# A graph-attention kernel on one core: third tile's masks ahead of the second table, x by rows in eight pieces, shorter flag

## The chip, the cores and the metric

One core of one Trainium2 chip. The metric is the device time of one execution in microseconds (us), as the median of three runs.

## What is computed

Cut to what matters (N = 4096 nodes, 128 channels, `adj` a 4096x4096 int32 matrix, sparse, of 64 MB):

```python
in_fts = W @ x.T
f1 = (w1 @ in_fts).T + b1              # one number per row
f2 = (w2 @ in_fts).T + b2              # one number per column
logits = f1 + f2.T                     # 4096 x 4096
bias = where(adj > 0, 0, -1e9)
coefs = softmax(leaky_relu(logits, 0.01) + bias, axis=-1)
y = x + coefs @ x
out = (y - mean(y)) / sqrt(var(y) + 1e-5)
```

## The kernel before

**The method.** leaky_relu has two slopes, so exp(leaky_relu(f1+f2)) is a product of a factor of the row and one of the column on either side of the sign of f1+f2. The kernel builds two tables of x scaled by the column's factor, `bt[:, 1]` ("minus", made first) and `bt[:, 0]` ("plus"), each with its low part beside it (258 columns, float16). For each tile of 128 rows it makes two masks of `adj`, one for each sign, and TensorE multiplies mask by table: 32 matmuls of 258 columns for each mask, 64 for a tile, 2048 for the 32 tiles (line 1091, `edge_sums`).

**One tile's way.** SyncE and ScalarE each load half of the tile's 2 MB (`load_near`, `load_far`, lines 277 to 280) into one of four buffers `nat`; the buffer is free again when the tile four back has been cast (`cast_done`). VectorE casts it to bytes (`cast`, L743), combines it with the signs that ScalarE makes (`signs`, L474, four instructions; `combine`, L748), transposes it (`turn`, L756: this is the minus mask) and derives the plus mask (`plus`, L761). TensorE sums both. ScalarE copies the sums out (`evacuate`, L616), and once per four tiles VectorE normalises (`moments`, L850 to L880), which reads x by rows, `xn`. Tiles 4 to 31 run so in loops, in pairs, each engine in program order.

**The start.** Tiles 0 to 3 are written out by hand in every engine's program, interleaved with the making of f2 (`f2_products` on VectorE, `f2_sums` on ScalarE, L495, two blocks of four columns by TensorE), f1 (`f1_columns` on TensorE from the transposed x; `spread_f1`, L710, on VectorE), the statistics (`turn_stats`, `widen_stats`, `stat_max`, `stat_out`), and the two tables. A table has four chunks; a chunk is scaled (`scale_x`, L732, on VectorE; `scale_act`, L518, or `scale_first`, L504, on ScalarE), its high part rounded by ScalarE (`split_x`, L542) and its low part formed by VectorE (`low_x`, L738). `gram` (L1103) sums squares of the minus table for a statistic. x itself lies in the storage of tile 2's and 3's masks (`xl` is `msk[:, 2:4]`), so `turn(2)` must come after chunk 1 of x has been used for both tables, `plus(2)` after chunk 0, `turn(3)` and `plus(3)` after chunks 3 and 2. The transposed x lies in the storage of `xn`, so x by rows can be loaded only after the last `f1_columns`.

**The order before** on VectorE (L792 to L839): scale minus chunks 0, 1; cast, combine tile 0; low 0; turn 0; scale 2; low 1, 2; f1; cast 1; low 3; combine 1; statistics; turn 1; scale plus chunks 2, 3; plus 0, 1 and low 0 to 3 of the plus table; then cast, combine, turn, plus of tile 2, and of tile 3. TensorE: tile 0 minus, gram, tile 1 minus, plus of tiles 0 and 1, then tile 2 minus (waits for `turn(2)`), and so on.

**x by rows and the flag.** GpSimd loads all of `xn` in four transfers of 512 KB (L379) once f1 is done and tile 1 is cast. GpSimd also computes whether the data's range allows the fast way, in twelve small operations after the rows' factors (L383 to L409), and writes `flag`; every engine reads it after its part of tile 3 (`fast`), SyncE already before it loads tile 7.

Of the kernel before, what the change touches and what calls it, by code (L numbers as in the profile page):

```python
# [16 lines left out]
P = 128  # L17
SQ = 32
# [24 lines left out]
def gat_kernel(nc, x, adj, W, w1, b1, w2, b2, out):  # L43
# [24 lines left out]
    with ExitStack() as ctx:  # L68
# [14 lines left out]
        junk = sb("junk", [P, KB * D], BF16)  # L83
# [70 lines left out]
        F2_PE = (0, 2)  # L154
        F2_AT = (FIRST * KB, NK - FIRST * KB)
# [6 lines left out]
        f2_made = sem("f2_made")  # L162
# [3 lines left out]
        y1_act = sem("y1_act")  # L166
        xl_in = [sem(f"xl_in{i}") for i in range(BCH)]
        xn_in = sem("xn_in")
# [119 lines left out]
        def _(sp):  # L288
# [8 lines left out]

            sp.dma_start(wsb[:, :], W).then_inc(w_in, 16)
# [8 lines left out]
            with sp.If(go):  # L307
# [23 lines left out]
            with sp.Else():  # L331
                for c in range(QT):
                    sp.wait_ge(nat_in[c], 16 * A * (2 if c < AHEAD else 1))
# [15 lines left out]
        def _(pool):  # L349
# [34 lines left out]
            pool.wait_ge(gst_ready, 2)  # L384
# [11 lines left out]
            pool.tensor_tensor(rng[:, 0:1], gst[:, 0:1], gst[:, 1:2], ALU.add).then_inc(rng_step, 1)  # L396
            pool.tensor_scalar(rng[:, 1:2], gst[:, 0:1], gst[:, 1:2], None, ALU.max).then_inc(rng_step, 1)
            pool.wait_ge(rng_step, 2)
            pool.tensor_tensor(rng[:, 1:2], rng[:, 1:2], gst[:, 2:3], ALU.add).then_inc(rng_step, 1)
            pool.tensor_scalar(rng[:, 0:1], rng[:, 0:1], F2_SPAN, None, ALU.is_le).then_inc(rng_step, 1)  # L400
            pool.tensor_scalar(rng[:, 2:3], gst[:, 3:4], (SCALE * X_MAX) ** 2, None, ALU.is_le).then_inc(rng_step, 1)
            pool.tensor_scalar(rng[:, 3:4], gst[:, 3:4], (SCALE * X_MIN) ** 2 * N, None, ALU.is_ge).then_inc(rng_step, 1)
            pool.wait_ge(rng_step, 6)
            pool.tensor_scalar(rng[:, 1:2], rng[:, 1:2], F_ABS, None, ALU.is_le).then_inc(rng_step, 1)
            pool.tensor_tensor(rng[:, 2:3], rng[:, 2:3], rng[:, 3:4], ALU.mult).then_inc(rng_step, 1)
            pool.wait_ge(rng_step, 8)
            pool.tensor_tensor(rng[:, 0:1], rng[:, 0:1], rng[:, 1:2], ALU.mult).then_inc(rng_step, 1)
            pool.wait_ge(rng_step, 9)
            pool.tensor_scalar(flag[:, :], rng[:, 0:1], rng[:, 2:3], None, ALU.mult).then_inc(flag_ready, 1)  # L409
# [47 lines left out]
        def _(act):  # L457
# [13 lines left out]
            def signs(t, c, between=None):  # L471

                for g in range(G):
                    ins = act.activation(sgn[:, c, g * JA:(g + 1) * JA], f2b[:, :], ACT.Sign,  # L474
                                         bias=nf1l[:, bass.ds(G * t + g, 1)], scale=-1.0)
                    if g == 1 and between:
                        between()
                ins.then_inc(sign_ready, 1)
# [6 lines left out]
            def f2_copy(i):  # L485

                b = F2_PE[i]
                bank, at = (0, F2_AT[0] + b * KB) if b < FIRST else (7, F2_AT[1] + (b - FIRST) * KB)
                act.wait_ge(f1_made if b < FIRST else f2_made, 1)
                act.activation(f2l[:, b * KB:(b + 1) * KB], ps[:, bank, at:at + KB], ACT.Copy).then_inc(f2l_act, 1)  # L490

            def f2_sums(n0, n1):
                act.wait_ge(xv_ready, 3)
                for n in range(n0, n1):
                    ins = act.activation(junk[:, (n - n0) * D:(n - n0 + 1) * D], xv[:, n * D:(n + 1) * D], ACT.Copy,  # L495
                                         accum_out=f2l[:, n:n + 1])
                ins.then_inc(f2l_act, 1)

            def scale_first(n0, n1):

                act.wait_ge(cs_ready[1], 1)
                for n in range(n0, n1):
                    h, i = n // CN, n % CN
                    ins = act.activation(ybuf[:, h, i], xl_chunk(h)[:, i], ACT.Copy, scale=cs[:, 1, n:n + 1])  # L504
                ins.then_inc(y1_act, 1)
# [27 lines left out]
            def split_x(m, h):  # L533
                if m == 0 and h < 2:
                    act.wait_ge(y_act, h + 1)
                elif m == 0:
                    act.wait_ge(y_ready[0], h - 1)
                elif h == BCH - 1:
                    act.wait_ge(y1_act, 2)
                else:  # L540
                    act.wait_ge(y_ready[1], h + 1)
# [6 lines left out]
            load_far(1, 1)  # L548
            xT_out(2)
            f2_copy(0)  # L550
            f2_sums(2 * CN, 2 * CN + KB)
            f2_copy(1)
            load_far(2, 2)
            act.wait_ge(b12_made, 1)
            act.activation(b12[:, :], ps[:, 6, D + 2:D + 3], ACT.Copy).then_inc(b12_ready, 1)
            act.wait_ge(f2l_ready, 4)
# [4 lines left out]
            scale_first(3 * CN, 3 * CN + KB)  # L561
            xT_out(4)
            act.wait_ge(f2b_ready, 1)
            act.wait_ge(nf1l_ready, 1)
            signs(0, 0, between=lambda: xT_out(5))
            load_far(3, 3)
            split_x(1, 0)
            xT_out(6)
# [3 lines left out]
            split_x(1, 1)  # L572
# [3 lines left out]
            scale_first(3 * CN + KB, NK)  # L576
            split_x(1, 2)
            signs(1, 1, between=lambda: split_x(1, 3))
            rows_out()
            scale_act(0)  # L580
            split_x(0, 0)
            act.wait_ge(cast_done, 2)
            load_far(QT + 1, 1)
            scale_act(1)
            split_x(0, 1)
            split_x(0, 2)
            split_x(0, 3)
            act.wait_ge(nf1l_ready, 2)
            signs(2, 2)

            def next_tile():
                act.wait_ge(cast_done, 3)
                load_far(QT + 2, 2)

            signs(3, 3, between=next_tile)
# [91 lines left out]
        def _(dve):  # L687
            def f2_products(i, n0, n1, s0=None):
# [6 lines left out]
                                  vsb[:, None, 0:D].to_broadcast([P, w, D]), ALU.mult).then_inc(xv_ready, 1)  # L695
                dve.wait_ge(xv_ready, i + 1)
# [38 lines left out]
            def low_x(m, h):  # L735
                part = slice(h * CN, (h + 1) * CN)
                dve.wait_ge(hi_ready[m], h + 1)
# [39 lines left out]
            f2_products(0, KB, 2 * KB)  # L777
            f2_products(1, 3 * KB, 4 * KB)
            f2_products(2, 2 * CN, 3 * CN, 2 * CN + KB)
            f2_products(3, 3 * CN, 4 * CN)  # L780
            dve.wait_ge(f2l_ready, 4)
            dve.wait_ge(f2l_act, 3)
            dve.tensor_reduce(stat[:, 0:1], f2l[:, :], AX_X, ALU.max)
            dve.tensor_reduce(stat[:, 1:2], f2l[:, :], AX_X, ALU.min, negate=True).then_inc(stat_ready, 1)
            dve.wait_ge(consts_ready, 2)
            dve.wait_ge(b12_ready, 1)
            spread_f1(0, 0, FIRST * KB, 0, 0)
            f2_rows()
# [228 lines left out]
        def _(pe):  # L1017
# [19 lines left out]
            def f1_columns(b):  # L1037
# [10 lines left out]
                if b == F2_PE[-1]:  # L1048
                    ins.then_inc(f2_made, 1)
# [168 lines left out]
```

## Time and profile before

| | us |
|---|---|
| median of 3 runs | 277.59 |
| the runs | 276.06 to 278.6 |
| the profiled execution, its own time | 275.19 |
| its span, first to last instruction | 273.5 |
| around the span | 1.7 |

An instruction's name is its line, engine and what it writes and reads; "idle before" is how long its engine had nothing to do ahead of it, and the arrow names what released it. TensorE has two rows, matmuls (PE) and weight loads (PEld), which overlap. The duration of a matmul in the rows is that from its start to its end, and several are in flight, so a rate is read from the time that a whole group takes.

### The profile page before, as it was taken

Reading aid. Unit: us, or ns where it says so; the run is one execution under the profiler, and the core shown is the slowest. Engines: PE = TensorE matmul, PEld = TensorE weight load, DVE = VectorE, ACT = ScalarE, POOL = GpSimd, SP = SyncE. Lnnn points to the kernel's source line nnn. Section 1 sums busy time; section 2 is a strip of 40 time slices with the busy share of each in tenths; the row PEclk is TensorE's granted clock in tenths of the full one; section 3 lists DMA queues with packets and bytes.
Section 4 is the critical chain, followed back from the end, with each engine's and each line's share of the span. In section 5 each row is a group of like instructions: output and inputs, shape, how many; then the busy total and the mean of one; then the engine's idle time right before and its main releaser. Section 6 shows DMA issues by size and latency. Waiting matters only on the chain.

```text
span 273.5 us, 5997 instructions
## 1 busy us (share of the span) xinstructions
PE 258.2 (94%) x2195; PEld 225.6 (82%) x2195; DVE 242.6 (89%) x309; ACT 195.6 (72%) x296; POOL 67.2 (25%) x98
## 2 busy tenths in 40 slices
PE   2999988799999999999999999999999999999991
PEld 2989877688888888888888888888888888888880
DVE  2888999988888899999999999999998999999963
ACT  2479999949999996999199919991999198003140
POOL 4002046930000006300630063006300630054150
PEclk9999999999999999999999999999999999999998
DMA  6999999999999999999999999999999999801011
GB/s 196 256 298 309 311 313 282 285 272 311 313 315 318 315 314 315 323 339 315 316 324 342 318 316 280 361 328 327 240 335 309 309 285 337 226 2 38 0 49 31
DMA packets 22562, 73.64 MB, mean 269 GB/s; under 512 B 3090, under 2 KB 4244, under 8 KB 22548
## 3 DMA queue, kind: packets, MB, share of 16 engines
q1 hardware_dynamic: 11184, 35.17, 42.9%
q10 hardware_dynamic: 9956, 34.64, 42.0%
q0 software_dynamic: 1408, 3.67, 4.7%
q8 instruction: 6, 0.10, 0.2%
q14 instruction: 8, 0.07, 0.1%
HBM read 71.37 MB, written 2.10 MB: 269 GB/s over the span
## 4 chain that ended last, share of the span: by engine, by line
DVE 58%; PE 16%; issue 8%; ACT 7%; DMA 7%; DVEq 1%; ACTq 1%; POOL 1%; POOLq 0%
DVE mn L743 19%; PE ps L1091 16%; DVE msk L756 11%; DVE mn L748 11%; DMA nat<-in_adj 5%; DVE post L855 3%; ACT sgn L474 3%; DVE ybt L870 2%; DVE bns L875 2%; ACT bt L542 2%; DVE ntot L860 2%; DVE post L857 2%; ACT post L518 2%; DMA msk<-in_x 2%; DVE mv L879 1%
## 5 line engine op out<-in xcount | busy, mean ns | idle before, releaser
L1091 PE MATMUL ps<-bt,msk 128*128 128x258 f16 x2048 | 232.1, 274 | 3.6 <-DVE msk L756 2.7
L1091 PEld LDWEIGHTS ps<-bt,msk 128*128 128x128 fp8e5 x2048 | 200.5, 98 | 34.2 <-issue 4.6
L474 ACT ACTIVATE sgn<-f2b,nf1l 128x1024 int8<-128x1024 f32 x128 | 136.4, 1144 | 5.2 <-POOL flag L409 4.0
L743 DVE TENSOR_SCALAR mn<-nat 128x4096 int8<-128x4096 int32 x32 | 73.1, 2284 | 5.0 <-DMA nat<-in_adj 4.6
L416 POOL TENSOR_SCALAR nmr<-mv 128x4 f32<-128x4 f32 x7 | 12.8, 1835 | 143.5 <-DVE mv L879 143.5
L756 DVE STREAM_TRANSPOSE msk<-mn 128x1024 uint32<-128x1024 uint32 x32 | 39.8, 1245 | 2.6
L748 DVE SCALAR_TENSOR_TENSOR mn<-sgn,mn 128x1024 uint32<-128x1024 uint32 x32 | 39.2, 1225 | 3.0 <-ACT sgn L474 2.0
L623 ACT ACTIVATE ybt<-ybt,nmr,rstd 128x128 f32<-128x128 f32 x28 | 11.5, 483 | 38.7 <-POOL nmr L421 38.7
L616 ACT ACTIVATE post<-ps,ac 128x258 f32<-128x258 f32 x60 | 24.8, 467 | 10.9 <-PE ps L1091 10.9
L761 DVE TENSOR_SCALAR msk<-msk 128x1024 uint32<-128x1024 uint32 x32 | 22.2, 695 | 1.0
L427 POOL DMA_DIRECT2D out<-ybt x24 | 13.7, 572 | 16.3 <-ACT ybt L623 14.9
L1047 PEld LDWEIGHTS ps<-vsb,xn 128*128 128x128 f32 x64 | 14.3, 332 | 0.5 <-issue 0.4
L1047 PE MATMUL ps<-vsb,xn 128*128 128x1 f32 (+1 forms) x64 | 13.9, 343 | 0.0
L1034 PE MATMUL ps<-ident,msk 128*128 128x128 f32 x32 | 8.6, 430 | 2.0 <-DMA msk<-in_x 2.0
L738 DVE SCALAR_TENSOR_TENSOR bt<-bt,post 128x1024 f16<-128x1024 f16 x8 | 9.6, 1223 | 0.6 <-ACT bt L542 0.6
L870 DVE SCALAR_TENSOR_TENSOR ybt<-ntot,rec,xn 128x128 f32<-128x128 f32 x28 | 8.0, 347 | 1.8 <-DVE rec L864 1.8
L542 ACT ACTIVATE bt<-post 128x1024 f16<-128x1024 f32 x8 | 8.2, 1051 | 0.6 <-DVE post L732 0.5
L855 DVE TENSOR_TENSOR post<-post 128x1032 f32<-128x1032 f32 x7 | 8.6, 1227 | 0.0
L1034 PEld LDWEIGHTS ps<-ident,msk 128*128 128x128 f32 x32 | 6.8, 248 | 2.1 <-DMA msk<-in_x 2.1
L482 ACT ACTIVATE xn<-ps 128x512 f32<-128x512 f32 x8 | 4.7, 594 | 4.7 <-PE ps L1034 4.7
L417 POOL TENSOR_SCALAR vpe<-mv 128x4 f32<-128x4 f32 x7 | 7.6, 1081 | 0.4
L419 POOL TENSOR_TENSOR rstd<-vpe,mhalf 128x4 f32<-128x4 f32 x7 | 7.5, 1064 | 0.6
(115 smaller groups left out, 105.2 us busy)
## 6 DMA issues: line engine op xcount, KB each, us to landing
nat<-in_adj SPq DMA_DIRECT2D x64, 512.0 KB, 15.1
nat<-in_adj ACTq DMA_DIRECT2D x64, 512.0 KB, 17.6
xn<-in_x POOLq DMA_DIRECT2D x4, 512.0 KB, 19.8
out<-ybt POOLq DMA_DIRECT2D x24, 64.0 KB, 6.6
msk<-in_x SPq DMA_DIRECT2D x8, 128.0 KB, 4.2
msk<-in_x ACTq DMA_DIRECT2D x8, 128.0 KB, 4.5
out<-ybt SPq DMA_DIRECT2D x4, 64.0 KB, 1.8
out<-post SPq DMA_DIRECT2D x4, 32.0 KB, 2.4
```

The lines of the kernel that those rows point to most:

```text
L427: pool.dma_start(out_g[q, g], ybt[g * SQ:(g + 1) * SQ, s]).then_inc(out_stored[s], 16)
L474: ins = act.activation(sgn[:, c, g * JA:(g + 1) * JA], f2b[:, :], ACT.Sign, bias=nf1l[:, bass.ds(G * t + g, 1)], scale=-1.0)
L542: act.activation(btv[m][:, h * CN:(h + 1) * CN, 0:D], ybuf[:, h], ACT.Copy, scale=1.0 / LOW).then_inc(hi_ready[m], 1)
L616: ins = act.activation(post[:, s, m, c, :], ps[:, 2 * c + m, 0:2 * DV], ACT.Copy, scale=ac[:, m, bass.ds(QT * q + c, 1)])
L743: dve.tensor_scalar(mn[:, c % 2], nat[:, c], 0, EDGE, ALU.is_gt, ALU.mult).then_inc(cast_done, 1)
L748: dve.scalar_tensor_tensor(out=mn_w[c % 2], in0=sgn_w[c], scalar=MINUS, in1=mn_w[c % 2], op0=ALU.bitwise_xor, op1=ALU.bitwise_and).then_in ...
L756: dve.transpose(turned[c].rearrange("p (b g s) -> p g b s", b=NB, g=G), mn_w[c % 2].rearrange("p (g b r) -> p g b r", g=G, b=NB)).then_inc ...
L761: dve.tensor_scalar(plus_w[c], turned[c], PLUS, 1, ALU.bitwise_and, ALU.logical_shift_right).then_inc(plus_ready, 1)
L855: dve.tensor_tensor(post[:, s, 0], post[:, s, 0], post[:, s, 1], ALU.add).then_inc(sums_added, 1)
L1034: ins = pe.transpose(ps[:, 4 + b % 2, k * P:(k + 1) * P], xl[:, n * D:(n + 1) * D], ident[:, :])
L1047: ins = pe.matmul(to, xT[:, n * P:(n + 1) * P], v, start=True, stop=True)
L1091: ins = pe.matmul(ps[:, 2 * c + m, 0:2 * DV], mask_f[c][m][:, n // KB, n % KB, :], btv[m][:, n, :], start=(n == 0), stop=(n == NK - 1))
```

## The change

It touches the start, the loading of x by rows and the flag. Tiles 4 to 31 keep their loops on TensorE, VectorE, ScalarE and GpSimd.

- VectorE scales all four minus chunks ahead of tile 0's cast (ScalarE's `scale_first` goes); `cast`, `combine`, `turn` of tile 2 come ahead of all low parts of the plus table, and the plus table's chunks are made in the order 1, 0, 2, 3, only chunk 0 scaled by ScalarE.
- TensorE does tile 2 minus ahead of all plus sums; these then go by chunks over the tiles; f1's columns and the sums of squares stand elsewhere; one block of f2 moves from TensorE to ScalarE.
- ScalarE makes tile 2's signs ahead of the plus table.
- x by rows goes by SyncE's queue, 256 KB for four tiles in four transfers, after the next four tiles' loads; SyncE's loop is written out.
- The flag takes eight operations, four of them after the last statistic.

The core of the diff:

```diff
@@ sync
+            def load_rows(q):
+                for g in range(G):
+                    sp.dma_start(xn[g * SQ:(g + 1) * SQ, QT * q:QT * (q + 1), :],
+                                 x_g[g][:, QT * q:QT * (q + 1)]).then_inc(xn_in[q % 2], 16)
+                sp.wait_ge(f1_made, 2)
                 load_quad(1, first=AHEAD)
-                load_quad(2)
-                load_quad(3)
-                with sp.Fori(2, NQ // 2) as turn:
-                    load_quad(2 * turn)
-                    load_quad(2 * turn + 1)
+                load_rows(0)
+                for q in range(2, NQ):
+                    load_quad(q)
+                    load_rows(q - 1)
+                sp.wait_ge(cast_done, NT - 1)
+                load_rows(NQ - 1)
@@ gpsimd
-            pool.wait_ge(f1_made, 2)
-            pool.wait_ge(cast_done, 2)
-            for g in range(G):
-                pool.dma_start(xn[g * SQ:(g + 1) * SQ, :, :], x_g[g]).then_inc(xn_in, 16)
@@ scalar
+            act.wait_ge(b12_made, 1)
+            (b12 copy)
+            f2_sums(1, CN)
+            load_far(1, 1)
+            f2_copy()
+            f2_sums(2, 2 * CN)
+            act.wait_ge(nf1_made, 1)
+            (nf1l copy)
+            xT_out(2)
+            load_far(2, 2)
...
-            scale_first(3 * CN, 3 * CN + KB)
...
+            signs(1, 1)
             rows_out()
+            act.wait_ge(cast_done, 2)
+            load_far(QT + 1, 1)
+            act.wait_ge(nf1l_ready, 2)
+            signs(2, 2)
+            split_x(0, 1)
             scale_act(0)
             split_x(0, 0)
-            scale_act(1)
+            act.wait_ge(cast_done, 3)
+            load_far(QT + 2, 2)
+            signs(3, 3, between={1: lambda: split_x(0, 2), 2: lambda: split_x(0, 3)})
@@ vector
             scale_x(1, 0)
             stat_max(0, 0, 2)
             scale_x(1, 1)
+            scale_x(1, 2)
+            scale_x(1, 3)
             stat_out(0, 0, 2)
             (nF2) cast(0) combine(0) low_x(1, 0) turn(0)
-            scale_x(1, 2)
             low_x(1, 1)
-            low_x(1, 2)
             spread_f1(1, FIRST * KB, NK, 7, 0)
             (xt1)
+            low_x(1, 2)
+            low_x(1, 3)
             cast(1) combine(1) (statistics) turn(1)
+            scale_x(0, 1)
+            stat_max(1, 2, 4)
+            cast(2, 2, 0)
+            stat_out(1, 2, 4)
+            combine(2, 2)
+            dve.wait_ge(y_ready[0], 1)
+            turn(2, 2)
+            plus(0, 0)
+            low_x(0, 1)
+            plus(1, 1)
             scale_x(0, 2)
+            low_x(0, 0)
             scale_x(0, 3)
+            plus(2, 2)
             low_x(0, 2)
             low_x(0, 3)
             cast(3) combine(3) turn(3) plus(3)
@@ tensor
             turn_x(0) turn_x(1)
+            (b12) f1_columns(0) f1_columns(1) turn_x(2)
             turn_x(3)
             (nf1, first part)
+            f1_columns(2)
             turn_x(4) turn_stats(0) f1_columns(3) turn_x(5) widen_stats(0) ...
+            minus_sums(0, 0)
             (nf1, second part) (xsum)
+            minus_sums(0, 1)
             gram(0) gram(1) gram(2) gram(3)
+            minus_sums(0, 2)
+            minus_sums(0, 3)
             (tile 1 minus)
+            edge_sums(2, 1)
+            plus_sums(ORDER[0], range(2))
+            plus_sums(ORDER[1], range(2))
+            plus_sums(ORDER[0], [2])
+            plus_sums(ORDER[1], [2])
+            plus_sums(ORDER[2], range(3))
+            plus_sums(ORDER[3], range(3))
             edge_sums(3, 1)
```

## Rows read from the trace of the kernel before

**Rows 1.** The page: 40 slices of the span, busy share in tenths.

```profile
PE   2999988799999999999999999999999999999991
DVE  2888999988888899999999999999998999999963
DMA  6999999999999999999999999999999999801011
```

**Rows 2.** Stretches: PE, PEld, DVE, ACT, POOL busy us (x); clock, DMA share, GB/s.

```profile
29.30:52.40 23.10, 19.52 (x168) 15.74 (x169) 21.69 (x25) 22.66 (x39) 11.87 (x17) 1.00 1.03 300
...
52.40:267.40 215.00, 214.96 (x1920) 187.44 (x1920) 197.88 (x249) 154.85 (x209) 49.63 (x63) 1.00 0.90 273
```

**Rows 3.** VectorE at the kernel's end: start us, us, what.

```profile
267.43 0.49 DVE L939 SCALAR_TENSOR_TENSOR post<-ps,ac,post 128x258 f32<-128x258 f32 x1 [2.14 <-PE ps L1091]
```

**Rows 4.** The chain that ended last: start us, us, what.

```profile
51.03 1.26 DVE msk L756
52.42 43.14 PE ps L1091 x384
```

**Rows 5.** Who waited for whom, 52 to 268 us: total, times, longest.

```profile
DVE mn L743 <- DMA nat<-in_adj: 4.0, 4, 1.1
ACT sgn L474 <- POOL flag L409: 4.0, 1, 4.0
...
PE ps L1091 <- DVE msk L756: 1.9, 1, 1.9
```

**Rows 6.** TensorE in order of time: start us, us, what.

```profile
6.38 1.97 PE L1034 MATMUL ps<-ident,msk 128*128 128x128 f32 x8 [2.01 <-DMA msk<-in_x]
...
26.02 3.41 PE L1047 MATMUL ps<-vsb,xn 128*128 128x1 f32 x16
...
29.30 3.60 PE L1091 MATMUL ps<-bt,msk 128*128 128x258 f16 x16
...
35.13 1.06 PE L1103 MATMUL ps<-bt 128*128 128x128 f16 x16
...
38.06 1.95 PE L1091 MATMUL ps<-bt,msk 128*128 128x258 f16 x16 [0.88 <-DVE msk L756]
```

**Rows 7.** VectorE in order of time, start of the kernel.

```profile
13.66 1.22 DVE L697 TENSOR_REDUCE f2l<-sgn 128x8 f32<-128x1024 f32 x1
...
16.10 2.02 DVE L702 STREAM_TRANSPOSE f2b<-f2l 128x1024 f32<-128x1024 f32 x1
...
18.00 1.20 DVE L732 TENSOR_TENSOR post<-msk,cs 128x1024 f32<-128x1024 f32 x1
...
19.12 0.27 DVE L719 TENSOR_REDUCE stmax<-ps 2x1 f32<-2x128 f32 x1
...
21.99 2.30 DVE L743 TENSOR_SCALAR mn<-nat 128x4096 int8<-128x4096 int32 x1 [0.58 <-DMA nat<-in_adj]
...
24.32 1.22 DVE L748 SCALAR_TENSOR_TENSOR mn<-sgn,mn 128x1024 uint32<-128x1024 uint32 x1
...
25.47 1.22 DVE L738 SCALAR_TENSOR_TENSOR bt<-bt,post 128x1024 f16<-128x1024 f16 x1
...
26.60 1.24 DVE L756 STREAM_TRANSPOSE msk<-mn 128x1024 uint32<-128x1024 uint32 x1
...
27.76 1.19 DVE L732 TENSOR_TENSOR post<-msk,cs 128x1024 f32<-128x1024 f32 x1
```

**Rows 8.** VectorE's mask operation, and ScalarE in order of time.

```profile
38.68 1.22 ACTq L280 DMA_DIRECT2D nat<-in_adj  x2
...
40.01 2.45 ACT L518 ACTIVATE post<-msk,cs 128x128 f32<-128x128 f32 x8 [0.28 <-issue]
...
42.26 0.67 DVE L761 TENSOR_SCALAR msk<-msk 128x1024 uint32<-128x1024 uint32 x1
...
42.49 2.95 ACT L542 ACTIVATE bt<-post 128x1024 f16<-128x1024 f32 x3
...
45.34 4.26 ACT L474 ACTIVATE sgn<-f2b,nf1l 128x1024 int8<-128x1024 f32 x4
```

More of the change, by code:

```diff
@@ L165, in gat_kernel @@
         den_step = sem("den_step")
-        y1_act = sem("y1_act")
         xl_in = [sem(f"xl_in{i}") for i in range(BCH)]
-        xn_in = sem("xn_in")
+        xn_in = [sem(f"xn_in{i}") for i in range(2)]
         nat_in = [sem(f"nat_in{i}") for i in range(QT)]
@@ L331, in _ @@
             with sp.Else():
+                sp.wait_ge(f1_made, 2)
+                for q in range(NQ):
+                    load_rows(q)
                 for c in range(QT):
@@ L469, in load_far, with signs @@
                     load_part(act, t, c, a)
-            def signs(t, c, between=None):
+            def signs(t, c, between={}):
                 for g in range(G):
@@ L475, in signs @@
                                          bias=nf1l[:, bass.ds(G * t + g, 1)], scale=-1.0)
-                    if g == 1 and between:
-                        between()
+                    if g in between:
+                        between[g]()
                 ins.then_inc(sign_ready, 1)
@@ L483, in xT_out, with f2_copy, f2_sums @@
                                accum_out=xt8[:, b:b + 1]).then_inc(xT_ready, 1)
[L485 to L495, printed above, removed]
+            def f2_copy():
+                act.wait_ge(f1_made, 1)
+                act.activation(f2l[:, 0:KB], ps[:, 0, FIRST * KB:FIRST * KB + KB], ACT.Copy).then_inc(f2l_act, 1)
+            def f2_sums(i, n0):
+                act.wait_ge(xv_ready, i + 1)
+                for n in range(n0, n0 + KB):
+                    at = ((i - 1) * KB + n - n0) * D
+                    ins = act.activation(junk[:, at:at + D], xv[:, n * D:(n + 1) * D], ACT.Copy,
                                          accum_out=f2l[:, n:n + 1])
                 ins.then_inc(f2l_act, 1)
[L499 to L505, printed above, removed]
             def scales(m, src):
@@ L695, in f2_products @@
                                   vsb[:, None, 0:D].to_broadcast([P, w, D]), ALU.mult).then_inc(xv_ready, 1)
+                if between:
+                    between()
                 dve.wait_ge(xv_ready, i + 1)
@@ L818, in _ @@
             dve.wait_ge(cs_ready[0], 1)
+            scale_x(0, 1)
[8 more added lines that the diff above has]
+            plus(1, 1)
             scale_x(0, 2)
-            stat_max(1, 2, 4)
+            low_x(0, 0)
             scale_x(0, 3)
-            plus(0, 0)
-            low_x(0, 0)
-            plus(1, 1)
-            stat_out(1, 2, 4)
-            low_x(0, 1)
+            dve.wait_ge(y_act, 1)
+            plus(2, 2)
             low_x(0, 2)
             low_x(0, 3)
-            cast(2, 2, 0)
-            combine(2, 2)
-            dve.wait_ge(y_act, 2)
-            turn(2, 2)
-            plus(2, 2)
             cast(3, 3, 0)
             combine(3, 3)
-            dve.wait_ge(y_ready[0], 2)
+            dve.wait_ge(y_ready[0], 3)
             turn(3, 3)
@@ L977, in _ @@
                 dve.wait_ge(g_f2_ready, 2 * A)
-                dve.wait_ge(xn_in, 16 * G)
+                for i in range(2):
+                    dve.wait_ge(xn_in[i], 8 * G * NQ)
                 STEPS = 7
@@ L1138, in _ @@
             edge_sums(1, 1, NK // 2, NK)
-            pe.wait_ge(den_ready[0], 1)
-            pe.wait_ge(xeps_ready, 1)
-            for h in range(BCH):
-                plus_sums(h, range(2))
             pe.wait_ge(xT_ready, NB)
@@ L1147, in _ @@
             edge_sums(2, 1)
-            for h in range(BCH):
-                plus_sums(h, [2])
+            pe.wait_ge(den_ready[0], 1)
+            pe.wait_ge(xeps_ready, 1)
+            plus_sums(ORDER[0], range(2))
[4 more added lines that the diff above has]
+            plus_sums(ORDER[3], range(3))
             pe.wait_ge(gst_ready, 2)
@@ L1154, in _ @@
             edge_sums(3, 1)
-            for h in range(BCH):
+            for h in ORDER:
                 plus_sums(h, [3])
@@ L1180, in _ @@
                 pe.wait_ge(g_f2_ready, 2 * A)
-                pe.wait_ge(xn_in, 16 * G)
+                for i in range(2):
+                    pe.wait_ge(xn_in[i], 8 * G * NQ)
                 with pe.Fori(0, NT) as t:
```

141 lines of the change are left out of this document (57 added, 84 removed).

## The prediction

> **What bounds the kernel now.** I read the slices of the span first: TensorE, VectorE and the DMA engines all stand at eight or nine tenths almost throughout [rows 1]. Only one of them can be the bound of a stretch, and the view by stretches tells which. From 52.40 to 267.40 us TensorE is busy 214.96 of 215.00 us with exactly 1920 matmuls, or 112.0 ns each; VectorE is busy 197.88 us of the same 215, the DMA engines 0.90 of it [rows 2]. One tile, 64 matmuls, costs 7.17 us all the way, and there are 30 tiles. A busy matmul row could hide waits, since several matmuls are in flight. But 16 whose inputs all lay ready took 1.95 us [rows 6], which is 112 ns from one to the next and one drain of some 0.15 at the end: the stream runs at the rate of matmuls that wait for nothing. Behind its last matmul come VectorE's step at 267.43 us and 6 us more [rows 3]. The chain that ended last enters the stream by tile 2's transpose at 51.03, then the matmuls from 52.42 [rows 4].
>
> The waits after 52 us say it from the other side: VectorE waited 4.0 us in all for tiles' data, ScalarE 4.0 us for the flag, TensorE only once, 1.9 us, for that transpose [rows 5]. What the change saves on the first two is worth nothing as long as TensorE's stream is never late. What can move the time is how much TensorE has done, and when, at the point from which it never waits again. From 29.30 to 52.40 us it is idle for 3.6 of 23.1 us [rows 2].
>
> **The change part by part.** (a) The measure. Before, TensorE enters its unbroken stream at 52.42 us with 128 matmuls done (tiles 0 and 1, both masks). After, it would enter it with tile 2's minus mask, with 64 done (tiles 0 and 1 minus), so 64 more are to come, 7.17 us. Break-even is a start at 52.42 - 7.17 = 45.25 us; the change gains or loses what it differs from that, provided that the plus tables and tile 3 then come in time.
>
> (b) VectorE up to tile 2's transpose. I lay its program out with the times from one start to the next in rows 7: cast to the dependent combine 2.33 us (21.99 to 24.32), cast to something independent 2.2 (estimate, 0.1 less), combine to the next 1.15, low part 1.13, turn to the next 1.16, scaling 1.13, a small statistic 0.1 to 0.3. The last f2 sum ended at 14.88; after, a small f1 operation stands in the middle, so 15.0. Then the 2.02 us transpose of f2 comes at once (it began at 16.10, behind statistics and a wait), two small statistics, and the first scaling at 17.2 instead of 18.00. There VectorE stops for TensorE to turn the statistic. TensorE: two turned blocks done at 8.35 [rows 6], then b12 0.4, two f1 blocks at 1.7 (16 instructions, two blocks, in 3.41 [rows 6]), two turned blocks at 0.9 and f1's first product: 14.6. ScalarE copies that and the third turned block, 15.45; f1 block 2 (1.7) and a turned block 0.9 follow, then the statistic: 18.5. Its reduction 0.45, three scalings 3.4, the returned statistic 0.3 bring tile 0's cast to 22.75. Before it was 21.99, where data ended the wait [rows 7]; 0.76 is lost here.
> From 22.75: cast 2.33, combine 1.15, low chunk 0 1.13, turn 0 1.16, low chunk 1 1.15 give 29.67. Now f1 must be complete: TensorE from 15.5 has six f1 blocks at 1.65, four turned blocks at 0.9, statistics 0.7, in all 14.2, seen by VectorE at 29.95; before, the last f1 column ended at 29.43 [rows 6]. Spread and small sum 0.32, low chunks 2 and 3 2.30: 32.57. Cast 1 2.33, combine 1.14, two statistics 0.29: 36.33. Turn 1 1.16, scale plus chunk 1 1.11, statistic 0.45: 39.05. Cast 2 2.20, copy 0.20, combine 1.33 (the turn depends on it), turn 1.25: **44.05 us**, against 52.29 before [rows 4]. Four low parts of the plus table (4.6), two masks (1.3) and one scaling net (1.1) went behind it.
> ScalarE must have the signs ready. Four take 4.26 [rows 8], 4.2 from the first start to the next operation. Tile 0's, with one copy between, run from 17.1 to 22.0, needed at 25.1. Tile 1's end at 32.7, needed at 34.9. Tile 2's stand behind two transfer issues that wait for cast 1 (34.9), 1.22 us [rows 8]: 36.15 to 40.4, needed at 41.45. The smallest cover is this 1.0 us.
>
> (c) TensorE up to there. Chunk 0 of tile 0 from 29.7 at the slow rate seen there, 16 in 3.60 [rows 6], so 8 in 1.8; f1's and x's sums 0.9; chunk 1 0.9 to 1.1 and 32 squares 1.9 (16 in 1.06 with a drain [rows 6]) end at about 35.5, needed at 36.1. The rest of tile 0 and the statistic to 37.6, tile 1 minus 2 x 1.8 and 0.5: 41.7. TensorE idles 2.4 us, and the stream starts at 44.1, against 45.25: **1.15 us gained**.
>
> (d) Does the stream hold? VectorE after 44.05: masks at 0.67 and turn, low and scaling as above [rows 7, 8]; ScalarE's scaling of a chunk 2.45, a high part 0.98 (three in 2.95) [rows 8]. Plus chunk 1 ready at 45.7 (needed 47.7), chunk 0 48.65 (49.5), tile 2's mask 50.4 (51.3), chunk 2 51.5 (53.1), chunk 3 52.7 (55.8). Tile 3's cast, combine, turn end at 57.5, needed at 44.1 + 128 x 0.112 = 58.4. So each is in time by 0.8 us or more; a stall of two microseconds on VectorE costs one. Then a tile takes VectorE 2.33 + 1.33 + 1.28 + 0.6 = 5.5 us against 7.17 and its cover grows.
>
> (e) x by rows. Four transfers of 512 KB at about 34 us go, 32 of 64 KB are spread over the stream; the bytes are the same. The 4.0 us of VectorE's waits for data may well go, but they lay under TensorE's stream: 0. Against it: the DMA engines are busy for 34 of 40 slices, to about 235 us, and fall off 30 us ahead of the end [rows 1], so the last tiles have room; 2 MB at 273 to 300 GB/s [rows 2] is 7 us. SyncE's additional issues, four of some 0.6 (half of 1.22 for two [rows 8]) for four tiles, stand behind loads already sent: 0. If both covers failed, the loss would be these 7 us less the room, 1 to 3. The last piece goes out with cast 31 under way and is used some ten us later: 0.
>
> (f) The flag comes some ten us earlier; ScalarE's wait of 4.0 us goes [rows 5]. It delayed tile 4's signs, for which TensorE never waited: 0.
>
> Sum: 275.19 - 1.15 = 274.0 for a profiled execution. The median of the runs stood 2.4 above the profiled one (277.59 against 275.19), so **276.4**, 0.4% faster. A measurement of this kernel tells about 1%, 2.8 us, from no change. Bounds: with no wait at all on VectorE and the cast at 21.99 again, the transpose would end at 43.0 and the gain be 2.3; with two covers missed by a microsecond each it would be 46, a loss of 0.8.
>
> **The clock.** The first 16 wide matmuls took 3.60 us, 16 later ones 1.95 [rows 6]: the lower and the higher of TensorE's two levels (1.2 and 2.4 GHz), although the granted clock of the stretch reads 1.00 [rows 2]. Ahead of the first 16 stood f1's single columns without a gap [rows 6], and they had not raised it. The change puts 8 wide ones there instead of 16, then narrow f32 work, and leaves a gap of 2.4 us at 41.7. The gap ahead of 52.42 was 1.9 us [rows 5] with the high rate on both sides. The Trainium skill ("TensorE: Matmul & The Clock Gate", its Part 1 and the table of advice at its end) says that a sustained busy stretch releases the clock and that a gap of idle sends it back; it would put the two places where the change is exposed at just these. For the gap the trace sides against a loss; for the rise no row decides.
>
> **The rivals.** *Slower: the clock rises late.* Were TensorE at the low level until tile 2: chunk 1 takes 1.75 and the squares 3.5 (32 at twice 55 ns, the 1.06 less its drain by 16), so the sum of squares is there at 37.7 and VectorE waits 1.6. The rest of tile 0 3.5, statistic 0.4, tile 1 minus 3.45 + 0.5 + 3.45 end at 48.8. The stream starts 3.55 behind break-even: 278.7, as a median 281.1. It costs from the point where the rise comes after about 37 us. For it: 8 wide matmuls instead of 16. Against it: TensorE hardly rests there. *No change: the start's chain slips.* The handovers in (b) late by 1.2 in all, f1's last block or the table's exponential behind transfer issues first: 277.6. For it: covers of 0 to 1 us. *Faster by more: waits are hidden in the matmul rows*, and VectorE's 4.0 us for data [rows 5] count: 277.6 - 4.0 = 273.6. Against it: one constant 112 ns. *Slower through the transfers:* small pieces in SyncE's queue slow a tile's load beyond 7.17 us: 1 to 3 us, 279.6 as a median. For it: DMA rows at nine; against it the 30 us at the end.
>
> **How the numbers follow.** Forecast 0.55, the slipped chain 0.22, late clock 0.09, transfers 0.05, faster by more 0.09. The likeliest one's own range is 275.2 (all bounds of (b) for it) to 277.2, and the runs' own spread (276.06 to 278.6 before) adds about 1 to either side. The range that leaves out 2 in 10 is 273.9 to 279.6. Faster by over 1% (below 274.8): the last case and a tail of the forecast, 0.13. Slower by over 1% (above 280.4): the late clock and a tail of the transfers, 0.11. Within 1%: 0.76.
>
> **What would show it.** Right: TensorE's matmuls run without a wait from about 44 us on, 1984 of them at 112 ns; one idle gap of about 2 us stands ahead; the waits at L743 and for the flag are gone, and yet the end has moved by a microsecond. Wrong in (b): tile 0's cast after 23.5, or f1 complete after 31. Wrong in (c): 16 wide matmuls in 3.4 us after 36 us. Wrong in (d): a second gap between 45 and 60 us. Wrong in (e): waits for `nat` that grow through the loop. The prediction as a whole is wrong if the stream's rate is no longer 112 ns.

## The result, and the profile after

The changed kernel takes 291.42 us (median of 6 runs, 288.81 to 292.29) against 276.82 (6 runs, 274.23 to 278.6) before: a ratio of 1.0527, with an interval of 1.0449 to 1.0605. The forecast was 276.4 us, 0.4% faster. The profiled execution took 291.62 us with a span of 290.0; before it was 275.19 with 273.5. So 16.5 us of span are to be explained. A ratio leaves out executions that stand over 1.5% above the fastest of their kernel and a median doesn't, so the two need not agree exactly.

From the page of the kernel after: the slices (busy share in tenths; GB/s moved), the queues (packets, MB, share of the DMA engines), the costliest groups, and the DMA issues with the time from issue to landing.

```profile
PE   3999979999999999999999999995999998995980
DMA  6999999999999999999999999999999999941102
GB/s 206 268 324 326 316 316 322 272 221 278 306 310 293 224 265 343 313 315 241 229 356 325 225 224 341 320 271 225 258 324 289 222 235 349 273 85 45 27 12 63
...
q1 hardware_dynamic: 15792, 37.26, 48.1%
q10 hardware_dynamic: 9956, 34.64, 42.2%
q0 software_dynamic: 832, 1.57, 1.8%
...
L1090 PE MATMUL ps<-bt,msk 128*128 128x258 f16 x2048 | 239.5, 279 | 9.9 <-DVE msk L747 9.9
...
L734 DVE TENSOR_SCALAR mn<-nat 128x4096 int8<-128x4096 int32 x32 | 73.1, 2284 | 22.8 <-DMA nat<-in_adj 22.5
...
nat<-in_adj SPq DMA_DIRECT2D x64, 512.0 KB, 15.8
nat<-in_adj ACTq DMA_DIRECT2D x64, 512.0 KB, 20.0
xn<-in_x SPq DMA_DIRECT2D x32, 64.0 KB, 24.2
```

And the queues of the kernel before, from its page (q1 is SyncE's, q10 ScalarE's, q0 GpSimd's; 73.64 MB in all, the same as after):

```profile
q1 hardware_dynamic: 11184, 35.17, 42.9%
q10 hardware_dynamic: 9956, 34.64, 42.0%
q0 software_dynamic: 1408, 3.67, 4.7%
```

VectorE's waits for the adjacency tiles went from 4.0 us [rows 5] to 22.5, TensorE's for masks from 1.9 to 9.9. The DMA slices stand at nine almost throughout, as before [rows 1], but the GB/s line has six dips to between 221 and 241, four or five slices apart, about one per quad, which is four tiles (29 us): busy engines, fewer bytes. The queue lines tell what is new. The 2.10 MB of x by rows have left GpSimd's queue (q0) and gone to SyncE's (q1). In q0 they had been 576 packets (1408 - 832), in q1 they are 4608 (15792 - 11184). Both numbers come apart as 16 packets for each transfer and the data: 4 x 16 + 512 packets of 4096 bytes before, 32 x 16 + 4096 of 512 bytes after, one for each row of x. The same bytes, eight times the packets.

TensorE after, in order of time from the start of its stream (start us, us, what, the idle time before it), then two stretches (PE busy us (instructions), granted clock, DMA share, GB/s):

```profile
43.91 152.32 PE L1090 MATMUL ps<-bt,msk 128*128 128x258 f16 x1344 [2.16 <-DVE msk L747]
199.74 45.77 PE L1090 MATMUL ps<-bt,msk 128*128 128x258 f16 x384 [3.51 <-DVE msk L747]
246.66 14.48 PE L1090 MATMUL ps<-bt,msk 128*128 128x258 f16 x128 [1.16 <-DVE msk L747]
264.27 17.28 PE L1090 MATMUL ps<-bt,msk 128*128 128x258 f16 x128 [3.12 <-DVE msk L747]
```

```profile
48.40:196.20 147.80, 147.80 (x1320) 1.00 1.04 284
196.20:281.60 85.40, 77.55 (x641) 0.92 0.76 197
```

Up to 196.2 us the stream has no gap and, from 48.4 us on, the old pace; then it breaks three times. The breaks cost 3.51 + 1.16 + 3.12 = 7.8 us idle. Behind the first and the third the matmuls are slower for a while: 384, 128 and 128 of them should take 43.0, 14.3 and 14.3 us at 112 ns and take 45.77, 14.48 and 17.28, 5.9 us more, nearly all of it behind the two gaps of over 3 us, at a granted clock of 0.92 over the whole stretch. Together 13.7 us. The rest of the 16.5 stands at the start (0.3, below) and behind the last matmul: the stream's end at 264.27 + 17.28 = 281.6 is 8.4 us before the end of the span, before it was 273.5 - 267.4 = 6.1. VectorE's last steps are late there, since its last cast began at 264.77 us instead of 247.61:

```profile
241.59 2.29 DVE L734 TENSOR_SCALAR mn<-nat 128x4096 int8<-128x4096 int32 x1 [5.19 <-DMA nat<-in_adj]
...
264.77 2.29 DVE L734 TENSOR_SCALAR mn<-nat 128x4096 int8<-128x4096 int32 x1
```

How do the packets slow the tiles? Eight microseconds in which a quad's rows of x are in SyncE's queue, by the DMA view of the kernel after, then the same stretch before:

```profile
DMA packets 866, 1.79 MB, mean 224 GB/s; under 512 B 97, under 2 KB 477, under 8 KB 865
...
q10 hardware_dynamic: 432, 1.57, 90.0%
q1 hardware_dynamic: 433, 0.21, 15.8%
```

```profile
q10 hardware_dynamic: 344, 1.26, 51.6%
q1 hardware_dynamic: 343, 1.25, 50.7%
```

Before, both hardware queues moved packets of 3.6 KB on average, 343 and 344 of them, 314 GB/s. After, the counts are again equal, 433 and 432, but SyncE's are mostly rows of 512 bytes. An equal count of packets with unequal sizes is what engines show that take one packet from each queue in turn. The half of each tile that stands behind the small packets doesn't move, and the other half cannot make up for it. The Trainium skill ("DMA: Bandwidth & Descriptors", section "Queues, rings and completion order") says that each DMA engine goes round the queues that have work, a packet at a time; the trace agrees, 433 against 432, if the Trainium skill means by a packet what the profile counts as one, which no run here shows.

TensorE takes a tile's 2.1 MB every 7.17 us, 293 GB/s, so at 224 the tiles fall behind. A reckoning from these rows: 380 packets of 512 bytes (477 - 97) in 8 us make a quad's 512 last 10.8 us. The rows of six quads, 0 to 5, stand ahead of tiles' loads in SyncE's queue (the dips are six as well); the last two quads' rows have no load of a tile behind them. Six times 10.8 us, each 90 GB/s below the 314 of before, are 5.8 MB short, 19 us at 314 GB/s. The 24 tiles that are loaded in that time need 6.7 us each of their 7.17 at 314 GB/s, which makes up for 12. Estimate: tiles' data 7 us late; TensorE's idle time in the loop was 7.8, and the slower matmuls behind two of its gaps added 5.9. The estimate is rough: with 301 GB/s between the dips, which the kernel after had from 104 to 112 us, the same sum gives 12.

### The profile page after: what moved, and what is told of

Read it like the earlier page. It is cut to its first block, busy times and chain, and to the rows that moved or that the text cites. A ratio compares the mean times of both kernels' runs of the same rounds, so it can differ in the third digit from the quotient of the medians.

```text
span 290.0 us, 5930 instructions
## 1 busy us (share of the span) xinstructions
PE 266.1 (92%) x2195; PEld 230.2 (79%) x2195; DVE 245.4 (85%) x310; ACT 192.6 (66%) x288; POOL 60.9 (21%) x91
## 2 busy tenths in 40 slices
DMA packets 26594, 73.64 MB, mean 254 GB/s; under 512 B 3538, under 2 KB 8788, under 8 KB 26580
## 3 DMA queue, kind: packets, MB, share of 16 engines
q1 hardware_dynamic: 15792, 37.26, 48.1%
## 4 chain that ended last, share of the span: by engine, by line
DMA 41%; DVE 19%; PE 15%; ACT 14%; issue 4%; ACTq 3%; POOL 2%; DVEq 0%; POOLq 0%
DMA nat<-in_adj 39%; ACT sgn L478 12%; PE ps L1090 6%; DVE mn L734 6%; PE ps L1047 5%; DVE mn L739 3%; PE ps L1034 3%; DVE msk L747 3%; ACTq L277 3%; ACT post L605 1%; DVE post L853 1%; DMA msk<-in_x 1%; DVE ybt L868 1%; DVE bns L873 1%; PE ps L1102 1%
## 5 line engine op out<-in xcount | busy, mean ns | idle before, releaser
L1090 PE MATMUL ps<-bt,msk 128*128 128x258 f16 x2048 | 239.5, 279 | 9.9 <-DVE msk L747 9.9
L1090 PEld LDWEIGHTS ps<-bt,msk 128*128 128x128 fp8e5 x2048 | 204.1, 100 | 44.2 <-issue 11.2
L734 DVE TENSOR_SCALAR mn<-nat 128x4096 int8<-128x4096 int32 x32 | 73.1, 2284 | 22.8 <-DMA nat<-in_adj 22.5
L431 POOL DMA_DIRECT2D out<-ybt x24 | 14.3, 594 | 15.8 <-ACT ybt L612 14.9
L723 DVE TENSOR_TENSOR post<-msk,cs 128x1024 f32<-128x1024 f32 x7 | 8.3, 1207 | 0.0
```

What stands on the lines that cost most here:

```text
L431: pool.dma_start(out_g[q, g], ybt[g * SQ:(g + 1) * SQ, s]).then_inc(out_stored[s], 16)
L734: dve.tensor_scalar(mn[:, c % 2], nat[:, c], 0, EDGE, ALU.is_gt, ALU.mult).then_inc(cast_done, 1)
L1090: ins = pe.matmul(ps[:, 2 * c + m, 0:2 * DV], mask_f[c][m][:, n // KB, n % KB, :], btv[m][:, n, :], start=(n == first), stop=(n == last - 1))
```

## The experiments

The theory was that the rows of x in SyncE's queue are the cause, with the new order of the masks as its rival. Two further rivals are SyncE's written-out loop, which experiment 1 keeps, and the idle time that the new order leaves on TensorE, which 4 and 9 fill. The expectations call the first A, with two readings that experiment 3 sets apart: A1, that the small packets hold SyncE's queue (above), and A2, that the number of transfers and of their issues does it. A3 and A4 are readings for experiment 5. Ratios are to the kernel before, run on the same chip.

**1. x by rows back on GpSimd's queue; all else as changed.**

```diff
+            pool.wait_ge(cast_done, 2)
+            for g in range(G):
+                pool.dma_start(xn[g * SQ:(g + 1) * SQ, :, :], x_g[g]).then_inc(xn_in, 16)
...
-                    load_rows(q - 1)
```

> The changed kernel with one part undone: x by rows is loaded again in four 512 KB transfers on GpSimd's queue (after f1 and tile 1's cast); everything else as changed. Theory A (the loss is the row pieces on SyncE's queue: from 174 us on TensorE waits for tiles' data): TensorE's stream holds 7.16 us a tile to the end, waits at the cast shrink from 22.5 to about 4 us or less, 276 to 278 us, ratio 1.00 with the clock's dip at 45 us still there. Rival B (the new order of the start costs, by whatever starves later): stays above 285. Rival C (the front was a gain that the transfers hid): 275.5, ratio 0.995.

275.14 us (12 runs, 273.3 to 276.54), ratio 1.0028 [1.0002, 1.0054]. All of the loss but 0.8 us is gone, with SyncE's loop still written out. B and C both fall. VectorE's waits for data, from 52 us on:

```profile
DVE mn L724 <- DMA nat<-in_adj: 3.9, 5, 1.0
```

**2. The kernel before with nothing but the 32 pieces of x in SyncE's queue.** The loop of the loads is written out as in the change.

> The kernel before with this one part alone: x by rows as 32 pieces of 64 KB on SyncE's queue behind each quad's tiles, SyncE's loop written out. Theory A: the whole loss comes with it, 288 to 292 us, a tile's data 7.7 us apart on average instead of 6.75. Rival B (it needs the new start as well): 277 to 280.

290.71 us (4 runs, 287.81 to 294.02), ratio 1.0567 [1.0498, 1.0636]. The whole loss comes with this part alone, and with it the waits, 19.7 us here:

```profile
DVE mn L751 <- DMA nat<-in_adj: 19.7, 9, 7.0
PE ps L1101 <- DVE msk L764: 10.2, 5, 3.7
```

The start as the cause falls. Packets and issues are still together.

**3. SyncE's queue, but all rows at once: 4 transfers of 512 KB.**

```diff
-                load_rows(0)
+                for g in range(G):
+                    sp.dma_start(xn[g * SQ:(g + 1) * SQ, :, :], x_g[g]).then_inc(xn_in, 16)
```

> The changed kernel with x by rows on SyncE's queue, but all at once as four transfers of 512 KB after tile 7's load instead of a quad at a time. Theory A1 (512-byte packets are taken one for one with the other queue's 4096-byte packets, and whatever stands behind them in SyncE's queue waits): 4096 packets at some 50 in a microsecond hold SyncE's queue for about 80 us, at 215 GB/s in all; near halves starve, TensorE stands still for tens of us, 300 us or more. Rival A2 (the many small transfers and their issue are the cost, not the packets): about as with GpSimd, 277 to 280.

292.12 us, one run, 17.8 above the kernel before on this chip. With four issues instead of 32 the loss is as large, so A2 falls. It comes as one stall, in which VectorE waits 23.41 us. Three stretches of the DMA view, 70 to 80, 90 to 96 and 102 to 108 us:

```profile
q10 hardware_dynamic: 560, 2.04, 88.7%
q1 hardware_dynamic: 555, 0.28, 15.8%
```

```profile
q1 hardware_dynamic: 2155, 1.28, 119.3%
q10 hardware_dynamic: 13, 0.03, 2.7%
```

```profile
DMA packets 337, 1.22 MB, mean 204 GB/s; under 512 B 38, under 2 KB 38, under 8 KB 337
```

First one for one again, 555 against 560 in 10 us. (In all, q1 has 15344 packets here: 4160 more than before, 4 x 16 and again 4096.) Once ScalarE's queue has run dry, SyncE's small packets pass some six times as fast, over 2000 in 6 us. That is why it isn't above 300 as A1 expected: it had left this out. It also shows that a small packet costs little by itself; what it costs is the turn of a large one. The third stretch is SyncE's queue alone with large packets: 204 GB/s, which is less than TensorE's 293.

**4. As 1, and TensorE's idle time ahead of tile 2's minus mask filled** with 18 matmuls whose result is overwritten.

```diff
+            for n in range(18):
+                pe.matmul(ps[:, 5, 0:2 * DV], mask_f[1][1][:, n // KB, n % KB, :], btv[1][:, n, :], start=True, stop=True)
```

> As r1, plus 18 matmuls whose result is overwritten, on TensorE between tile 1's minus mask and the wait for tile 2's transpose, where it idled 2.2 us. Theory (the idle gap lets the clock fall at 45 us, 28 matmuls at 215 ns follow): no matmul over 130 ns after 36 us, the stream has 128 done at about 51.1 instead of 52.7 us, 1.5 us faster than r1. Rival (the dip comes from the sparse start, not from the gap): the dip stays, time as r1 or 0.2 slower.

273.58 us (12 runs, 272.89 to 276.06), ratio 0.9983 [0.9961, 1.0006]. TensorE in order of time, of the kernel after, then of this one; and the stretch of 7.17 us from the stream's start, in the same order:

```profile
39.79 1.96 PE L1090 MATMUL ps<-bt,msk 128*128 128x258 f16 x16
43.91 6.27 PE L1090 MATMUL ps<-bt,msk 128*128 128x258 f16 x40 [2.16 <-DVE msk L747]
```

```profile
39.78 1.96 PE L1078 MATMUL ps<-bt,msk 128*128 128x258 f16 x16
41.59 2.17 PE L1130 MATMUL ps<-bt,msk 128*128 128x258 f16 x18
43.82 10.35 PE L1078 MATMUL ps<-bt,msk 128*128 128x258 f16 x91
```

```profile
43.91:51.08 7.17, 7.17 (x50) 0.76 1.03 320
```

```profile
43.82:50.99 7.17, 7.17 (x65) 1.00 1.03 294
```

After an idle time of 2.16 us the granted clock reads 0.76 and 50 matmuls pass; without the idle time 1.00 and 65. Within the 0.76 it is at its lower level, 1.2 GHz, for 3.35 us of the kernel after:

```profile
44.95:48.30 3.35, 3.35 (x18) 0.50 1.02 313
```

Fifteen matmuls of 112 ns are 1.7 us. (So some 15 to 18 matmuls passed slowly, not the 28 of the expectation.) The medians of 1 and 4 differ by 1.56, but the intervals of their ratios touch.

Such a gap does not always lower the clock. Kernel 3 has the start of the kernel after and idled there even longer, 2.31 us, and its stream has the full rate:

```profile
43.20 50.28 PE L1082 MATMUL ps<-bt,msk 128*128 128x258 f16 x448 [2.31 <-DVE msk L741]
```

```profile
43.20:50.37 7.17, 7.17 (x65) 1.00 1.02 314
```

Of the five profiled executions with this gap four show the dip (2.16, 2.24, 2.28 and 2.22 us, in the kernel after, 1, 5 and 6) and 3 does not; of those with the gap filled none does. Later in their streams gaps of 2.31 us in 2 and 2.40 in 5 left the clock at 1.00 too, and those of 2.60 us and more were all followed by the lower level. So the gap is needed for the dip, but between 2.16 and 2.40 us its length alone does not decide. What else does stays open.

**5. Two of each quad's four pieces on ScalarE's queue.**

```diff
-                for g in range(G):
+                for g in range(G // 2):
...
+                        if c == 1:
+                            rows_far(q, s)
```

> The changed kernel with each quad's four row pieces divided: two on SyncE's queue as changed, two on ScalarE's queue right behind the far half of the same quad's last tile. Same bytes, same 512-byte packets. Theory A3 (only while small packets stand in one hardware queue against 4096-byte packets in the other do they cost much, since the other queue alone moves some 210 GB/s; where both queues carry them at once they go quickly): more than half of the loss goes, 277 to 284 us. Rival A4 (a 512-byte packet costs the same in either queue): 288 to 292 us, as the changed kernel. Rival (the halves' times don't overlap, and now both halves of a tile are late): 291 or more.

287.56 us (4 runs: 282.8, 287.19, 287.93, 290.93), without a ratio; the profile is that of the longest. The hope was that small packets of both queues would pass each other. In the profile they stood at different times: at 92 to 96 us SyncE's 222 packets (0.12 MB) beside ScalarE's 223, 237 GB/s in all, at 100 to 104 ScalarE's 205 (0.23 MB) beside SyncE's 214, 258 GB/s. Each held up its own half of a tile, and VectorE's waits came to 23.2 us. The median lies above the 277 to 284 of A3 and just under the 288 of A4, but the fastest execution lies inside A3's range, so the times do not decide between the two. What the profile shows is that the condition of A3, small packets in both queues at once, was not met.

**6. The same 32 pieces at the same places, but 2048 contiguous bytes per partition.** This takes other rows of x into the residual than the computation asks for; nothing else is changed.

```diff
-                    sp.dma_start(xn[g * SQ:(g + 1) * SQ, QT * q:QT * (q + 1), :],
-                                 x_g[g][:, QT * q:QT * (q + 1)]).then_inc(xn_in[q % 2], 16)
+                    sp.dma_start(xn.rearrange("p t d -> p (t d)")[g * SQ:(g + 1) * SQ, QT * q * D:QT * (q + 1) * D],
+                                 x_flat[q, g * SQ:(g + 1) * SQ]).then_inc(xn_in[q % 2], 16)
```

> The changed kernel with another source for x by rows: the same 64 KB pieces at the same places of SyncE's queue to the same places of xn, but from 2048 contiguous bytes for each partition (the residual then adds wrong rows of x; the time is what is looked at). 128 packets of 2048 bytes a quad instead of 512 of 512. Theory A (the number of packets counts, each waiting its turn against one of the other queue): the queue is held for a quarter of the time, 3 us instead of 11, a quad's data take 28 us or less against TensorE's 28.6, 275 to 278 us. Rival (bytes, pieces, issue or SyncE's written-out loop count): 288 to 292 us.

280.37 us (4 runs, 276.81 to 281.63), ratio 1.0134 [1.0047, 1.0221]. Issues, queue, places and bytes are those of the change; the packets of the rows are a quarter as many (q1 has 12720, 1536 more than before: 32 x 16 and 1024). Most of the loss goes with them: three quarters by the ratios, three fifths by the medians (280.37 is 5.8 above this chip's 274.58, the change lost 14.6); the ratio's interval allows for 58 to 91%. The time is 2 us above theory A's range and 8 below the rival's. One more thing differs, the rows' places in memory, now one block for each piece; that the scattered rows are not what costs is shown by 1 and 7, which read the same rows on GpSimd's queue at ratios of 1.0028 and 1.0016. TensorE's stretch and VectorE's end of this run:

```profile
52.40:267.40 215.00, 214.82 (x1921) 1.00 0.94 272
```

```profile
254.45 2.29 DVE L735 TENSOR_SCALAR mn<-nat 128x4096 int8<-128x4096 int32 x1
...
272.22 0.49 DVE L938 SCALAR_TENSOR_TENSOR post<-ps,ac,post 128x258 f32<-128x258 f32 x1
```

In this stretch TensorE is never without work. But the last cast begins at 254.45 us instead of 247.61, and VectorE's last step, which had waited 2.14 us for TensorE [rows 3], comes with no wait at 272.22 instead of 267.43. The tiles' data may be late by that one slack and no more; this is a second way in which transfers cost time, at the end alone.

**7. As 4, with the rows a quad at a time on GpSimd's queue**, in GpSimd's loop.

```diff
+            def load_rows(q, s):
+
+                for g in range(G):
+                    pool.dma_start(xn[g * SQ:(g + 1) * SQ, bass.ds(QT * q, QT), :],
+                                   x_g[g][:, bass.ds(QT * q, QT)]).then_inc(xn_in[s], 16)
```

> The kernel of r4 (changed, idle gap filled) with x by rows on GpSimd's queue, but a quad at a time inside its loop instead of all at 35 to 65 us. Theory A (the queue and its packets were the cost, not the spreading over time): as r4, 273 to 274.5 us, ratio 0.998 within 0.003, and VectorE's early waits for tiles' data (3 to 4 us) gone without any gain. Rival (spreading itself costs): 277 or more. Rival (those waits do count after all): 270.

275.22 us (12 runs, 274.39 to 276.13), ratio 1.0016 [0.9991, 1.0041]. The pieces of 64 KB as such are nearly free once their queue is not a tile's. Its queue q0 has 1856 packets for the 3.67 MB, 1024 above the 832 of the kernel after: 32 x 16, and 512 of 4096 bytes, so the pieces are packed here too. The time is 0.7 us above the expected range. The waits for data are not gone, as had been hoped for with the spread; they are more than in 4 (3.1, 3, 1.1):

```profile
DVE mn L731 <- DMA nat<-in_adj: 6.5, 5, 1.6
```

The last cast begins at 248.87 us, in 4 at 246.18. This need not be a property of the pieces: the profile of 10, which is kernel 4 once more, has 5.5 us of these waits and its last cast at 249.41 (below), and those of 7 and 10 are both among the longest of their kernel's runs (276.13 and 276.93 us). The intervals of 7 and of 4 overlap, so whether the spread costs anything was not measured.

**8. As 4, and 14 wide f16 matmuls in TensorE's idle time from 1.7 to 6.4 us**, to raise the clock early.

```diff
+            fill(5)
...
+            fill(9)
```

> The kernel of r4 with 14 more matmuls of 256 f16 columns whose result is not used, 5 and 9 of them, in TensorE's idle time before x arrives (1.7 to 6.4 us). Theory (wide matmuls raise the clock and the f32 work behind them keeps it up): f1's instructions come every 107 ns instead of 213, f1 is complete some us before 29 us, VectorE's three waits for TensorE at the start (0.57, 0.29, 0.51 us) go, the stream starts 1 us earlier, ratio 0.994. Rival (the f32 work does not hold the clock, or so few wide ones don't raise it): starts 213 ns apart as before, time as r4 within 0.3 us.

273.95 us (12 runs, 272.72 to 276.97), ratio 0.9993 [0.9964, 1.0022]. Nothing is gained, beside 0.9993 for kernel 4 on the same chip (10). The single columns and the wide matmuls behind them take what they took without it (3.41 us for 16 before [rows 6], 1.88 for 8 in the kernel after):

```profile
25.99 3.41 PE L1035 MATMUL ps<-vsb,xn 128*128 128x1 f32 x16
29.26 1.88 PE L1086 MATMUL ps<-bt,msk 128*128 128x258 f16 x8
```

**9. As 4, with 9 matmuls instead of 18**, so that 1.06 us stay idle.

```diff
-            for n in range(18):
+            for n in range(9):
```

> The kernel of r1 with 9 instead of 18 matmuls in the idle gap ahead of tile 2, so that 1.1 us of it stay idle. Theory (the length of idle time there decides, and the 1.9 us ahead of 52.42 in the kernel before were survived): the clock stays up, time as r4. Rival (any idle time there lets it fall): the dip of 28 matmuls at 215 ns is back, time as r1.

274.59 us (10 runs, 273.29 to 275.47), ratio 1.0004 [0.9979, 1.0028]. The stream's first 7.17 us:

```profile
43.65:50.82 7.17, 7.17 (x65) 1.00 1.04 281
```

Idle for 1.06 us the clock stays, in this one profile. The profile says this at once; the medians of 4 and 9 on this chip (below) can't be told apart.

**10. Kernel 4 once more**, beside 8 and 9.

> The kernel of r4 once more, on the same chip as r8 and r9: ratio 0.998 to the kernel before, within 0.002; this decides whether the changed start with x by rows on GpSimd's queue and the gap filled is a gain or none.

274.18 us (12 runs, 273.21 to 277.03) beside 274.27 before (29 runs), ratio 0.9993 [0.9964, 1.0021]. The best version found is as fast as the kernel before, to within what can be measured. Its profiled execution took 276.93 us. From VectorE's order of time:

```profile
249.41 2.29 DVE L724 TENSOR_SCALAR mn<-nat 128x4096 int8<-128x4096 int32 x1
...
267.19 0.48 DVE L927 SCALAR_TENSOR_TENSOR post<-ps,ac,post 128x258 f32<-128x258 f32 x1
```

The last cast is late and the last step comes without a wait for TensorE, as in 6, although here no small packets stand in SyncE's queue beyond those of the kernel before. The same kernel has the wait of 2.14 us in 4. The slack behind the last tile is so small that it is there in one execution and gone in the next.

## Why the prediction was wrong

**(a) to (c), the start, were right in what they traced.** Tile 0's cast came at 21.90 us (forecast 22.75), f1 was complete at 29.18 (29.95), the turn of tile 2 ended at 43.77 (44.05), the stream began at 43.91 (44.1), 1.3 us ahead of break-even. TensorE's idle time ahead of it was 2.16 us (2.4).

**The clock: this sentence failed, at a price of 1.7 us.** "For the gap the trace sides against a loss" rested on the 1.9 us gap before [rows 5], behind which the rate stayed. Behind 2.16 us it fell: 50 matmuls instead of 65. The 1.3 us gained were lost again to 1.7 of slower matmuls, and the stream stood 0.3 us later than before instead of 1.15 earlier. Kernels 4 and 9 show that without the full gap there is no dip, kernel 3 that with it there need not be one (2.31 us idle, 65 matmuls). The forecast's trace had only one gap, 0.3 us shorter; a single safe case was read as a rule. The Trainium skill ("TensorE: Matmul & The Clock Gate", the table of its section "Why this matters for your kernels") asks for no idle gaps above a certain length, one that 2.16 us doesn't reach; here the measurement decides, and that gap was enough in four executions of five.

**(d), the stream behind the start, held**: not a gap from 43.91 to 196.2 us. No mask or table of tiles 2 and 3 was late.

**(e), x by rows at nothing: this is the step that failed, with all of the loss but some 0.8 us** (of 14.6 between the medians; kernel 1 stands 0.83 above the kernel before). "The bytes are the same" was true, and the wrong measure. What counts is packets in the queue of a tile's half, and there the change put eight times as many as GpSimd's queue had needed for the same bytes. Kernels 1 and 2 place the whole loss in this part, 3 rules out the number of issues, 6 shows the packets' size to carry most of it. The term came to 14.6 us where the prediction had 0. "If both covers failed, the loss would be 1 to 3" failed as well: it priced the bytes that are left over at the end, not a rate of 224 GB/s for 10.8 us out of 28. (Nor does the 1 to 3 follow: 7 us less a room of 30 is nothing.) Both covers named were no covers. The room at the end [rows 1] is in good part built up in the loop, by 0.5 us per tile, 2 us per quad (7.17 less the 6.7 at 314 GB/s); the small packets cost 3 us per quad (19 by 6), so it was never built, and by 196 us the lead of the start was used up. The GB/s of the loop [rows 2] is a mean over both queues; no row that was read gave a packet's size or a single queue's pace. The queue lines of the page, 11184 packets for 35.17 MB beside 1408 for 3.67, were there and were not used.

**(f), the flag, was right at 0**: it came at 43.82 us, and ScalarE's wait for it is gone. In 4, with x by rows back on GpSimd's queue, the wait is back with 4.9 us, and TensorE's stream has no gap there either.

**The rivals.** The fourth, "small pieces in SyncE's queue slow a tile's load beyond 7.17 us", is what happened, with a chance of 0.05 and a price of 1 to 3 us; the term was mis-sized, by a factor of about five against its upper end. (Its 279.6 adds 2 us to the time before, 277.6, and not to the forecast; and the late clock's steps add up to 49.0, not 48.8. Neither changes the picture.) "Waits for `nat` that grow through the loop" had been named as its sign, and 22.5 us of them are there. The late clock came in small part: chunk 1 took 1.93 us at the low rate and the 32 squares 2.62, where the forecast had 0.9 to 1.1 and 1.9 and the rival 1.75 and 3.5; VectorE waited 0.51 us for them, and the stream began on time all the same. The slipped chain did not come either. Waits hidden in the matmul rows are refuted by 4: its waits for data fell from 4.0 to 3.1, the time stayed.

Open is why the unbroken stream breaks first at 196 us and then at uneven distances; what decides whether a gap of some 2.3 us lowers the clock; and how what is left in 6 divides between the packets of 2 KB and the place of the rows among the loads.

## What to carry to other kernels

When a transfer is moved to another queue, count its packets beside its bytes: the queue lines of the page give both, and while small packets stand in a queue that feeds the bound, that queue moved here one of them for each large packet of its neighbour. Rows of 512 bytes belong on a queue that packs them or that nobody waits for, or must be laid out to be long. And where a step is bought with a gap on TensorE, fill the gap, or count a possible low rate behind it (1.7 us here) against the gain.

## What was unexpected of the hardware

GpSimd's queue carried rows of 512 bytes as packets of 4096, SyncE's as packets of one row each (512 against 4096 packets for 2.10 MB). SyncE's queue alone gave 204 GB/s with large packets, both hardware queues together 314. Small packets pass six times as fast when the other queue is empty: over 2000 in 6 us against some 550 in 10 beside large ones. And an idle time of 2.16 us lowered TensorE's clock, where 1.06 us did not, nor 1.9 in the kernel before, nor 2.31 in kernel 3 at the same place: the same gap is followed by the lower level in one execution and not in another.
